# An adaLN transformer block on one core: Pool's order in the second normalisation, where the reload stands in the transfer queue, and W_base by half tiles

## The reference

```python
# x: (2, 1024, 1024); sa, ca, ga, sb, cb, gb: six vectors per batch from silu(c) @ wmod (wmod 1024 x 6144)
h = layernorm(x) * (1 + ca) + sa
q, k = rotary(h @ wq), rotary(h @ wk);  v = h @ wv          # 32 heads of 32
x = x + ga * (softmax(causal(q k^T / sqrt(32))) v @ wo)
h = layernorm(x) * (1 + cb) + sb
base = h @ W_base^T + b_base
gate = softmax(h @ W_gate^T);  thr = sigmoid(h @ W_thr + b_thr) / 8
w = max(gate - thr, 0), divided by its sum                   # 8 experts
x = x + gb * (base + 2 * sum_e w_e * (h @ A_e^T) @ B_e^T)    # rank 16
```

## Time and profile before

| | us |
|---|---|
| median of 3 runs (1723.79 to 1727.38) | 1724.31 |
| the profiled execution | 1725.72 |
| its span, first to last instruction | 1723.9 |
| PE busy in the span | 1611.1 (93%) |
| DVE busy | 1015.7 (59%) |
| ACT busy | 960.1 (56%) |
| POOL busy | 605.5 (35%) |
| mean granted PE clock | 0.972 |

### The profile page before, as it was taken

How to read it: one execution, slowest core, us unless ns; L and a number is a source line. 1 busy time by engine, 2 the same in 40 slices (tenths; PEclk the granted TensorE clock), 3 DMA queues, 4 the chain that set the end, 5 groups by cost and what they waited for, 6 DMA issues and landing times. The chain is left out here.

```text
span 1723.9 us, 29774 instructions
## 1 busy us (share of the span) xinstructions
PE 1611.1 (93%) x9530; PEld 1183.2 (69%) x9530; DVE 1015.7 (59%) x3292; ACT 960.1 (56%) x2296; POOL 605.5 (35%) x475
## 2 busy tenths in 40 slices
PE   5888989999899989999999999997889999999996
PEld 2556766666667757777777777774468888888885
DVE  5627676667667647667567666665355354544533
ACT  2336777867778767787887878777621010111100
POOL 3533243443424324233243243330413433434342
PEclk9999999999999989999999999997699999999998
DMA  9583433435353274323322432322561112121210
GB/s 348 204 255 85 99 100 101 109 93 131 83 147 87 59 225 126 90 68 79 98 72 69 98 82 56 90 63 73 132 197 37 58 52 73 37 74 47 63 57 29
DMA packets 170722, 174.46 MB, mean 101 GB/s; under 512 B 20890, under 2 KB 120522, under 8 KB 170580
## 3 DMA queue, kind: packets, MB, share of 16 engines
q1 hardware_dynamic: 168468, 168.54, 35.2%
q10 hardware_dynamic: 2112, 4.19, 0.7%
HBM read 96.65 MB, written 25.18 MB: 71 GB/s over the span
## 5 line engine op out<-in xcount | busy, mean ns | idle before, releaser
L1466 ACT ACTIVATE rows_sb<-rows_sb,bias_m 128x640 f32<-128x640 f32 (+7 forms) x512 | 396.4, 775 | 222.6 <-DVE bias_m L1751 222.3
L1733 DVE CUSTOM_DVE_ANT_0 rows_sb<-ps_t,mask 128x512 f32<-128x512 f32 (+3 forms) x512 | 295.5, 585 | 156.8 <-PE ps_t L1233 148.6
L1502 ACT ACTIVATE probsT<-ps_s 128x512 f32<-128x512 f32 (+2 forms) x640 | 319.8, 546 | 9.5 <-PE ps_s L1264 7.1
L1233 PE MATMUL ps_t<-stk 96*128 96x512 f32 (+3 forms) x768 | 274.5, 361 | 28.8 <-DVE smax L1733 19.6
L1264 PE MATMUL ps_s<-stk 98*128 98x512 f32 (+3 forms) x768 | 237.4, 389 | 17.4 <-ACT probsT L1502 10.7
L1774 DVE TENSOR_TENSOR ps_s<-ps_s,mask_t 128x128 f32<-128x128 f32 (+1 forms) x384 | 120.6, 339 | 156.4 <-PE ps_s L1264 155.0
L1264 PEld LDWEIGHTS ps_s<-stk 98*128 98x128 f32 x768 | 134.4, 196 | 108.4 <-issue 49.3
L1233 PEld LDWEIGHTS ps_t<-stk 96*128 96x128 f32 x768 | 148.3, 193 | 86.3 <-DVE smax L1733 28.2
L1901 POOL TENSOR_TENSOR rope_b<-rope_b,rope_sin 128x512 f32<-128x512 f32 x64 | 82.8, 1293 | 315.9 <-DVE rope_b L1718 315.9
L1291 PE MATMUL ps_pv<-probsT,v_all 128*32 128x256 f32 (+1 forms) x2816 | 187.7, 360 | 1.2 <-ACT probsT L1502 1.2
L1222 PE MATMUL ps_qkv<-hT_hi,w_hi 128*128 128x512 f32 x384 | 159.0, 414 | 6.4 <-DVE hT_lo L1693 2.9
(11 more groups left out here) (199 smaller groups left out, 3042.3 us busy)
## 6 DMA issues: line engine op xcount, KB each, us to landing
stk<-rot SPq DMA_DIRECT2D x384, 128.0 KB, 2.4
probsT<-in_L_wmod_dram SPq DMA_DIRECT2D x5, 2048.0 KB, 11.3
wm_one<-in_L_wmod_dram SPq DMA_DIRECT2D x5, 2048.0 KB, 14.4
w_raw<-in_L_attn_wq_dram SPq DMA_DIRECT2D x16, 512.0 KB, 4.2
w_raw<-in_L_attn_wk_dram SPq DMA_DIRECT2D x16, 512.0 KB, 4.6
w_raw<-in_L_attn_wv_dram SPq DMA_DIRECT2D x16, 512.0 KB, 4.5
attn_scratch<-attn_sb SPq DMA_DIRECT2D x128, 64.0 KB, 3.1
a_raw<-attn_scratch SPq DMA_DIRECT2D x16, 512.0 KB, 4.8
```

The costliest lines, as they stand in the source:

```text
L1233: pe.matmul(bank[:, 0:c1 - c0], stk[0:3 * HD, u % 2, 0, qt // 4, h, qt % 4 * P:(qt % 4 + 1) * P], stk[0:3 * HD, u % 2, 1, part, h, 0:c1 - ...
L1466: act.activation(row, row, ACT.Exp, bias=bias_m[:, qt, h:h + 1], scale=SCALE, accum_out=sums[:, qt // 4, h, qt % 4:qt % 4 + 1]).then_inc(s ...
L1502: act.activation(probsT[:, w % 4, hs[0]:hs[-1] + 1, 0:n], s_bank[(NS * u + k) % 3][:, 0:len(hs) * n].rearrange("p (h n) -> p h n", h=len(hs)),
L1733: dve.tensor_tensor_reduce(rows_sb[:, to, at + c0:at + c1], bank[:, 0:n], mask[:, BANK - n:BANK] if last else mask[:, 0:1].broadcast_to([P ...
```

## The change

Seven edits. (1) POOL does `ln_rstd` and `next_rest` ahead of `rope_total` in a slot. (2) The normalisation of a tile moves from slot 2 to slot 3. (3) ACT does `next_round` ahead of the slot's row exponentials and scores' exponentials. (4) The first half of `hT_lo` is issued behind `stack(14, 1)` and `place_m(13, 1)`. (5) Behind the rows of half period 0 stand 5, then 2, then 4 products, and the rotation of chain (1, 0) begins at row 20. (6) wo is loaded into buffers of the second normalisation (`x_next`, and `h_next` joined with `h_next_hi` as `h_pair`), without the waits for the weight buffers. (7) The weight pieces are loaded by half tiles (256 KB) into eight stages of 512 columns. Their order becomes: the first halves of the eight W_base pieces, the six halves of the others, the second halves of W_base. The first eight units (`SOON`) are loaded in u = 30, turned by PE in slots 1 to 8 of u = 31 into the two banks of the chains, and rounded and rested by DVE in slots 2 to 9; the next eight are loaded by SP within u = 31, each once DVE has finished the unit whose stage it takes; six more follow in phase B. There the three parts are six, three and five units.

```diff
-NORM_STEPS = {1: "stats", 2: "norm", 6: ("turn", 0), 7: ("scale", 0), 8: ("split", 0), ...
+NORM_STEPS = {1: "stats", 3: "norm", 6: ("turn", 0), 7: ("scale", 0), 8: ("split", 0), ...
-BEHIND = [5] * EARLY_ROWS + [3] * (NR - EARLY_ROWS)
+BEHIND = [5] * EARLY_ROWS + [2] * 8 + [4] * 8
-FIRST_M0, FIRST_V = 13, (5, 10)
+FIRST_M0, FIRST_V, FIRST_ROPE = 13, (5, 10), 20
...
-        wo_raw = [w_flat[:, i * D:(i + 1) * D] for i in range(2)]
+        wo_raw = [x_next[:, :], h_pair[:, :, :].rearrange("p a n -> p (a n)")]
-        stage = [gb[:, 0, :], gb[:, 1, :], bias[:, :], spare[:, :]]
+        stage = [x[:, a * BANK:(a + 1) * BANK] for x in (gb[:, 0, :], gb[:, 1, :], bias[:, :], spare[:, :]) for a in range(2)]
...
-        items = [("ag", 0), ("ag", 1), ("bt", 0)] + [("wb", o) for o in range(KT)]
+        UNITS_ = [("wb", o, 0) for o in range(KT)] + [(kind, k, half) for kind, k in (("ag", 0), ("ag", 1), ("bt", 0))
+                                                      for half in range(2)] + [("wb", o, 1) for o in range(KT)]
+        UNITS, SOON = len(UNITS_), KT
-        parts = [slice(0, 4), slice(4, 6), slice(6, len(items))]
+        parts = [slice(SOON, SOON + 6), slice(SOON + 6, SOON + 9), slice(SOON + 9, UNITS)] + [
+            slice(n, n + 1) for n in range(SOON)]
...
+        def turn_weights(pe, part):
+            for n, kind, k, half, bank in turned(part):
+                if n == SOON:
+                    pe.wait_ge(max_ok, NR * PAIRS)
+                    pe.wait_ge(m_ok, 2 * PAIRS)
+                    pe.wait_ge(at_ok, 2 * PAIRS)
+                elif n == 0:
+                    pe.wait_ge(vT_ok, 2 * T)
+                pe.wait_ge(st_ld[n % len(stage)], loaded[n])
+                if SOON <= n < SOON + len(turn_bank):
+                    pe.wait_ge(st_lo, SOON)
+                elif n >= 2:
+                    pe.wait_ge(st_lo, n - 1 if n < SOON else n - len(turn_bank) + 1)
+                ...  four transposes into bank
+        def rest_weights(dve, part):
+            for n, kind, k, half, bank in turned(part):
+                ...
+                if n < SOON:
+                    dve.wait_ge(st_t, n + 1)
+                    dve.tensor_copy(hi, turns).then_inc(st_hi, 1)
+                dve.wait_ge(st_hi, n + 1)
+                dve.tensor_tensor(lo, turns, hi.bitcast(F32), ALU.subtract).then_inc(st_lo, 1)
...
@@ sync
             for u in range(PAIRS):
-                if u == 2 * G - 3:
-                    load_next_hT(0)
                 if u + 1 < PAIRS:
                     sp.wait_ge(st_ok, NS * u)
                     stack(u + 1, 1)
                 place_m(u, 1)
+                if u == 2 * G - 3:
+                    load_next_hT(0)
...
                 if u == PAIRS - 3:
-                    sp.wait_ge(qk_hi_ok, 4 * T)
-                    sp.wait_ge(qk_lo_ok, 4 * T)
-                    sp.wait_ge(v_hi_ok, 2 * T)
-                    sp.wait_ge(v_lo_ok, 2 * T)
                     for k in range(2):
                         load_wo(k)
...
                 if u == PAIRS - 1:
                     load_wo(6)
                     load_wo(7)
+                    for n in range(len(stage), 2 * len(stage)):
+                        load_piece(sp, n)
@@ tensor, after the chain, the turns and the rows of slot i
+                    if u == PAIRS - 1 and 0 < i <= SOON:
+                        turn_weights(pe, 2 + i)
@@ scalar, slot i
                         next_out(step[0], step[1][1], q_bank[chain_left(u, i)[1] % 2])
+                    if step and step[1][0] == "split":
+                        next_round(step[0], step[1][1])
                     ...  copy_v, row_exps, softmax_exp, copy_vT, round_m
-                    if step and step[1][0] == "split":
-                        next_round(step[0], step[1][1])
@@ vector
-            rope_products(1, 0)
+                    if k == FIRST_ROPE:
+                        rope_products(1, 0)
...
                     if i in DIAGS:
                         triangle(u, i)
+                    if u == PAIRS - 1 and 1 < i <= SOON + 1:
+                        rest_weights(dve, 1 + i)
@@ gpsimd, slot i
                     if (u, i) in ROUND_AT:
                         rest_rot(*ROUND_AT[u, i])
-                    if (u, i) in ROPE_AT:
-                        rope_total(*ROPE_AT[u, i])
                     ...  ln_rstd in the "stats" slot, next_rest in the "split" slot
+                    if (u, i) in ROPE_AT:
+                        rope_total(*ROPE_AT[u, i])
```

More of the change, by code:

```diff
@@ L439, in adaln_block @@
         at_st = [sem("at_st0"), sem("at_st1")]
-        st_ld = [sem(f"st_ld{i}") for i in range(4)]
+        st_ld = [sem(f"st_ld{i}") for i in range(8)]
         wo_ld = [sem(f"wo_ld{i}") for i in range(3)]
@@ L566, in load_early @@
             sp.wait_ge(proj_mm, 6 * T)
-            for i in range(len(stage)):
-                load_piece(sp, i)
+            for n in range(len(stage)):
+                load_piece(sp, n)
         def load_a(sp, i):
@@ L574, in phase_b_sync @@
         def phase_b_sync(sp):
-            def load_pieces(some):
-                for i in some:
-                    sp.wait_ge(st_lo, units_to[i - len(stage)])
-                    load_piece(sp, i)
             def load_x(i, e):
@@ L592, in phase_b_sync @@
             load_x(0, 0)
-            load_pieces(range(len(stage), len(items)))
+            for n in range(2 * len(stage), UNITS):
+                load_piece(sp, n)
             load_x(1, 1)
@@ L614, in phase_b_sync @@
             sp.wait_ge(out_st, 16 * B * NT)
+        def turn_weights(pe, part):
[11 more added lines that the diff above has]
+                    pe.wait_ge(st_lo, n - 1 if n < SOON else n - len(turn_bank) + 1)
+                rows = piece_cols(kind, k)
+                for j in range(4):
+                    mm = pe.transpose(bank[:, j * rows:(j + 1) * rows], stage[n % len(stage)][0:rows, j * P:(j + 1) * P],
+                                      ident[0:rows, 0:rows])
+                mm.then_inc(st_t, 1)
@@ new lines, in rest_weights @@
+        def rest_weights(dve, part):
+            for n, kind, k, half, bank in turned(part):
+                rows = piece_cols(kind, k)
+                hi, lo = piece(kind, k, half)
+                turns = bank[:, 0:4 * rows].rearrange("p (k n) -> p k n", k=4)
+                if n < SOON:
[3 more added lines that the diff above has]
+                dve.tensor_tensor(lo, turns, hi.bitcast(F32), ALU.subtract).then_inc(st_lo, 1)
@@ L616, in phase_b_tensor @@
         def phase_b_tensor(pe):
             pe.wait_ge(at_ok, 2 * PAIRS)
-            def turn_weights(part):
-                for n, i, kind, k, half, bank in turned(part):
-                    if n == 0:
-                        pe.wait_ge(max_ok, NR * PAIRS)
-                        pe.wait_ge(m_ok, 2 * PAIRS)
-                        pe.wait_ge(vT_ok, 2 * T)
-                    if half == 0:
-                        pe.wait_ge(st_ld[i % len(stage)], loaded[i])
-                    if n >= len(turn_bank):
-                        pe.wait_ge(st_lo, n - len(turn_bank) + 1)
-                    rows = piece_cols(kind, k)
-                    for j in range(4):
-                        kt = 4 * half + j
-                        mm = pe.transpose(bank[:, j * rows:(j + 1) * rows], stage[i % len(stage)][0:rows, kt * P:(kt + 1) * P], ident[0:rows, 0:rows])
-                    mm.then_inc(st_t, 1)
@@ L849, in body @@
                     dve.tensor_tensor(x1[:, e, cols], x1[:, e, cols], xn[:, cols], ALU.add).then_inc(last_ok, 1)
-            def rest_weights(part):
-                for n, i, kind, k, half, bank in turned(part):
-                    rows = piece_cols(kind, k)
-                    hi, lo = piece(kind, k, half)
-                    dve.wait_ge(st_hi, n + 1)
-                    dve.tensor_tensor(lo, bank[:, 0:4 * rows].rearrange("p (k n) -> p k n", k=4),
-                                      hi.bitcast(F32), ALU.subtract).then_inc(st_lo, 1)
             dve.wait_ge(wo_lo_ok, KT)
-            rest_weights(0)
+            rest_weights(dve, 0)
             dve.wait_ge(rows_ld, 16 * (B + 1))
@@ L865, in phase_b_vector @@
             norm(0, 0)
[L866 to L867 removed]
+            rest_weights(dve, 1)
+            rest_weights(dve, 2)
             modulate(0, 0)
@@ L966, in store_next @@
                 sp.wait_ge(ln_lo, NT + 2 * tt + half + 1)
-                for a, part in enumerate((h_next_hi[:, :].bitcast(F32), h_next[:, :])):
+                for a, part in enumerate((h_next_hi, h_next)):
                     sp.dma_start(h_dram[a].rearrange("(k p) t -> p k t", p=P)[
@@ L1405, in next_out @@
                     act.wait_ge(h_st, 32 * (2 * tt + half))
-                act.copy(h_next[:, :], bank).then_inc(h_cp[half], 1)
+                act.copy(h_next, bank).then_inc(h_cp[half], 1)
             def next_round(tt, half):
                 act.wait_ge(h_mod[half], tt + 1)
```

(2 more changed lines are left out.)

59 lines of the change are left out of this document (27 added, 32 removed).

## The result

The changed kernel takes 1707.6 us (median of 4 runs, 1704.73 to 1709.38) against 1724.05 for the kernel before (4 runs): ratio 0.9899, 95% interval 0.988 to 0.9918, so 16.5 us less. The forecast was 1700.5 us. The profiled executions are 1706.75 and 1725.72 us, their spans 1704.9 and 1723.9: 19.0 us apart.

A forecast was written before the change was run, and what follows sets the result against it. PE was taken to bound nearly all of phase A. Gains 13.0 + 4.0 + 0.3 - 1.5 + 8.0 = 23.8 us turn 1724.31 into 1700.5 us, range 1690 to 1712.

The forecast's parts named there:

- the reload: Half period u = 13: maxima land earlier, cost falls from 9.7 to 5.7 us, gain 4.0; bounds -3.2 and +7.7.
- Normalisation: Pairs of half periods with normalisation: fewer PE waits and a better clock, gain 13.0 us; bounds 4.3 and 16.8.
- The waits that go: In normalised pairs, four PE waits of 1.97 us for maxima (7.9) and the waits for ACT's copy (5.9) vanish.
- The clock: In normalised pairs, PE's clock of 0.98 recovers: 1.5 us back, bounds 0 and 3.0.
- what is late next: Normalisation in slot 3 ahead of slot 4's maxima: 6.5 us of DVE, 2.3 taken as cost, bounds 0 and 6.5.
- The warning on slot 3: Normalisation in slot 3 can meet POOL's rest of weights; four even half periods would pay 1.0 us more each on DVE.
- The bandwidth, not the order, decides: Reload in u = 13: 5.0 MB at 292 GB/s take 17.1 us from 611.8, landing at 628.9.
- The second rival: Reload lands late: -3.2 us instead of +4.0, total gain 16.6, 1707.7 us; chance 0.12.
- First rows: Half period 0: the 1.27 us wait for the rotation goes, another may grow; +0.3 us, bounds -1.4 and +1.3.
- Last half period: Eight weight units turned there, mostly in PE's idle time: cost 1.5 us; bounds cost 7.0 and gain 1.0.
- Between the phases: Fewer weight units and no wait for a W_base transfer in part three: gain 8.0 us, bounds 3.0 and 9.0.
- Its own signs: Trace checks: listed waits gone, normalised pairs 72 to 73 us, 36 us between phases; wrong if probsT waits grew.

The follow-up runs named there:

- Experiment 10: Kernel before with POOL's deviation and rest ahead of the rotation and ACT's rounding first, normalisation still in slot 2: 1712.61 us, ratio 0.9928.
- Experiment 3: Kernel before with only ACT's rounding first and POOL's rest of a half ahead of the rotation: 1720.81 us, ratio 0.9974.
- Experiment 2: Kernel before with only the normalisation moved from slot 2 to slot 3: 1717.83 us, ratio 0.9954.
- Experiment 5: Changed kernel with hT_lo issued again at the top of u = 13, ahead of the stack and the row of maxima: 1707.52 us, ratio 0.99.
- Experiment 8: Changed kernel with the reload's first 512 columns all on SP's queue and a semaphore for each half of k-tiles: 1708.59 us, ratio 0.9905.
- Experiment 9: Experiment 8 plus ACT's two transfers in slot 5 instead of 6 and the stack for u = 15 ahead of SP's second reload: 1699.87 us, ratio 0.9854.
- Experiment 12: Experiment 11 with the first rows' old product counts and the rotation of chain (1, 0) after all rows: 1700.46 us, ratio 0.9849.
- Experiment 7: Changed kernel with the reload's first 512 columns all on SP's queue, ACT's two other transfers in slot 6 instead of 4: 1714.59 us, ratio 0.9939.
- Experiment 1: Kernel before with POOL's new order, the normalisation in slot 3 and ACT's rounding first, nothing else: 1714.15 us, ratio 0.9938.
- Experiment 11: Experiment 9 with the normalisation back in slot 2: 1699.87 us, ratio 0.9839.

## Why the prediction came out as it did

The direction and the range held; the forecast was 7 us too low, 23.8 us of gain against 16.5 by medians. Four of its five terms had the sign of what was measured or were too small to tell, and the reload had the wrong one. By its steps:

- **Normalisation, forecast 13.0, measured 10.3** (9.7 in the eight and 0.6 in u = 10). The waits that go were sized right: 18.0 to 10.1 and 5.9 to nothing. The clock gave 3.4, where 1.5 was taken and 3.0 was the bound. The term that was mis-sized is what is late next: 2.3 us were set against it, and 3.5 (turning of maxima) + 3.4 (exponentials, 4.7 less 1.3) = 6.9 came, a little over the bound of 6.5. The step put all of it down to the normalisation in slot 3 and to the maxima of slot 4. Of the 6.9 us only 2.1 go with slot 3 (exponentials 4.7 with it, 2.6 in Experiment 10 without); the 3.5 come with edit 3 (Experiment 3), which the step had as free. And it took edits 1 and 2 as one cause; they are substitutes (Experiments 2 and 10), and with the first in place the second costs 1.6.
- **The warning on slot 3 came true in small:** 1.44 against 0.81 us, 0.6 for each of four instead of 1.0, and Experiment 10 shows that slot 2 avoids it. The three rows shown (1.80, 1.44 and 1.02 us) all end 0.54 to 0.56 us after the POOL instruction beside them, whenever they began. The Trainium skill, SBUF — State Buffer, section "SBUF: two separate sides", calls the port pair that DVE and GpSimd share an exclusive lock, held for a whole instruction; the traces agree.
- **The reload, forecast +4.0, measured -1.6 by the pair of profiles and -2.7 by Experiment 5.** This is the step that failed. "The bandwidth, not the order, decides" was its premise, with the first bytes at 611.8 and the last at 628.9. On that time base (11.5 us added to the changed kernel's) the stack was issued at 614.1, its first bytes moved at 615.1, and hT_lo landed at 633.7: 3.3 us of the 4.8 are the late start, the rest is that the same 5 MB took 18.6 us and not 17.1. The stack had been counted at the full rate, and the order did matter, since SP could issue hT_lo only behind the row of maxima, at 608.11, and PE needed the whole of it. Nor did the wait for the row of maxima go: PE stood 2.13 us for it and 5.64 for h, in place of 4.0 in all. The second rival (-3.2) had the sign and the late transfer right, and about twice the size; its bound rested on a landing 19.0 us after the issue, which was hT_hi's, while hT_lo had taken 10.7 and now took 14.1. That its total of 1707.7 us is the measured median is luck, since its other terms were off. The time could be had, 9.8 us of it, with the order by need and by halves (Experiments 8 and 9).
- **First rows, +0.3: nothing measurable** (Experiment 12). The 1.27 us at 141.17 went; the row's wait grew from 1.42 to 1.67, and that for the turning of the maxima behind the rows from 1.43 to 1.63.
- **Last half period, -1.5:** from the first to the last matmul of scores 24.6 before and 24.7 us in the changed kernel; over all profiles 23.6 to 24.6 without the units and 23.2 to 27.1 with them, means 24.0 and 24.9. A cost of about 1, not resolved. B_w's 16 issues took 9.7 us and the last store went out some 1.5 us late, covered as said.
- **Between the phases, +8.0: 7.8 in the pair**, part three 4.3 us, "some 36" from the attention's end 36.0. Together with the last half period 5 to 8 us were measured, 6.5 forecast.
- **Unforecast:** 1.9 us in phase B, which belongs to the one profile of before and not to the change. It is part of why the spans differ by 19.0 and the medians by 16.5.
- **Its own signs:** no wait for maxima near 2.0 us, none for h_next and the 36 us came out. The normalised pairs took 73.7 us for 72 to 73, the wait for m_rows stayed, a W_base transfer stayed in the chain, and "waits for probsT grown", named as a sign of being wrong, came true (1.3 to 4.7 us).

10.3 - 1.6 + 1.3 (u = 1 begins so much sooner in the pair) - 0.1 + 7.8 + 1.9 - 0.4 (u = 29 and 30) = 19.2, against 19.0 of the spans. The 1.3 is no gain of edit 5: the first product of a row comes 1.95 us sooner in the changed kernel's profile, and from there to u = 1 it takes 0.6 longer.

## What to carry to other kernels

When a stall of PE is removed, look at what it had hidden: PE comes sooner to the next producer, and a good part of the gain may stand there as a new wait (3.5 of 5.9 us in Experiment 3). Ask of two edits with one aim which would do alone; here the slot did (Experiment 2), the earlier deviation did (with edit 3, Experiment 10), and both together were worse than the deviation without the slot. A bulk reload is ordered by need and in pieces that have their own semaphores, for the half period after it too: in Experiment 8, 6.4 of the 10.1 us that u = 13 gained were lost again in u = 14. And when an edit moves two transfers, look for the loss in the next half period as well before naming its cause: all of Experiment 7's was there.

## What the runs showed of the hardware that was not expected

- A transfer from SBUF to SBUF over 32 partitions moved 196 GB/s with the queue to itself, one from HBM to 128 partitions 387. One queue alone moved h at the same 380 to 400 whether it was SP's or ACT's, and both queues with h together at 377; it was some 280 where a stack was under way.
- A normalisation (128 x 1024, DVE) takes 0.81 us alone. In the seven profiles read for it (the kernel before, the changed one, Experiments 1, 2, 3, 10 and 11) 31 of them began beside a POOL instruction of 1.3 us, 0.02 to 1.20 us after its start. Thirty ended 0.55 us after POOL's, and the one that began last, with 0.11 us of it left, took 0.81. So each paid what was left of POOL's instruction, less some 0.26 us.
- The same work between u = 30 and the first tile took 96.3 us in the changed kernel and 101.2 in Experiment 9, at a granted clock of 0.74, 0.87 and 1.00 in its three stretches against 0.61, 0.76 and 0.95. Nothing in the code differs there; PE, with idle time in this place, was given the upper level at different times, and the same matmuls kept it busy 6.0 us longer. Single runs of one kernel spread as much: Experiment 9's go from 1696.76 us at a mean granted clock of 0.981 to 1705.08 at 0.974. That is larger than edits 4 and 5, and a likely reason why the medians of Experiments 9 and 11 don't show the 1.6 us by which the eight differ in the traces. The rows, first the changed kernel:

```profile
1178.60:1212.00 33.40, 25.48 (x141) 13.69 (x140) 20.22 (x76) 25.84 (x63) 7.09 (x3) 0.74 0.46 137
1212.00:1238.00 26.00, 19.40 (x157) 11.86 (x156) 15.04 (x32) 18.64 (x36) 13.56 (x6) 0.87 0.56 135
1238.00:1274.90 36.90, 30.50 (x165) 24.62 (x165) 18.03 (x30) 9.30 (x18) 6.21 (x6) 1.00 0.61 193
```

```profile
1171.70:1206.10 34.40, 27.84 (x139) 15.48 (x139) 20.63 (x76) 25.18 (x60) 7.09 (x3) 0.61 0.44 134
1206.10:1235.00 28.90, 22.00 (x159) 12.87 (x158) 15.05 (x32) 18.81 (x37) 14.09 (x6) 0.76 0.52 123
1235.00:1272.90 37.90, 31.59 (x160) 25.55 (x160) 18.12 (x30) 9.29 (x18) 5.64 (x5) 0.95 0.57 186
```
